# Leaving out the filler matmul ahead of each unit's transposes in a neighbourhood-attention stage

## What is computed

```
qkv = (layernorm(x) @ qkv_w + qkv_b)            # q is scaled by hd ** -0.5
attn = einsum('nhijc,nhiajbc->nhijab', q, kwin) + bias
attn = softmax(attn over the 7 x 7 window)
out = einsum('nhijab,nhiajbc->nhijc', attn, vwin)
x = x + out @ proj_w + proj_b
x = x + gelu(layernorm(x) @ fc1_w + fc1_b) @ fc2_w + fc2_b
```

## Time and profile before

| what | value |
|---|---|
| median of 3 runs | 598.47 us (598.18 to 599.26) |
| the profiled execution | 598.55 us |
| its span, first to last instruction | 596.7 us |
| TensorE busy in the span | 518.5 us (87%) |
| VectorE busy | 407.5 us (68%) |
| ScalarE busy | 312.2 us (52%) |
| mean granted TensorE clock | 0.947 |

### The profile page before, as it was taken

How to read it: one execution, slowest core, us unless ns; L and a number is a source line. 1 busy time by engine, 2 the same in 40 slices (tenths; PEclk the granted TensorE clock), 3 DMA queues, 4 the chain that set the end, 5 groups by cost and what they waited for, 6 DMA issues and landing times.

```text
span 596.7 us, 10777 instructions
## 1 busy us (share of the span) xinstructions
PE 518.5 (87%) x4207; PEld 278.9 (47%) x4208; DVE 407.5 (68%) x740; ACT 312.2 (52%) x456; POOL 57.8 (10%) x108
## 2 busy tenths in 40 slices
PE   6898889875899999999999999999999562799871
PEld 5565666641344454444444444444444220366621
DVE  5785676677766568778966886767662456898662
ACT  2764558550365655565556555565556243565440
POOL 8161244211010000100000010000000100000000
PEclk9999999997799999999999999999999966999975
DMA  5101000000000000000000000000000000000001
GB/s 112 41 2 37 1 2 1 2 2 0 1 1 1 1 1 2 1 2 1 0 1 2 2 0 2 11 0 2 1 1 1 1 3 14 1 1 1 1 0 36
DMA packets 9897, 4.37 MB, mean 7 GB/s; under 512 B 8948, under 2 KB 9207, under 8 KB 9847
## 3 DMA queue, kind: packets, MB, share of 16 engines
q1 hardware_dynamic: 8566, 3.66, 2.7%
q10 hardware_dynamic: 1281, 0.01, 0.1%
HBM read 2.09 MB, written 0.52 MB: 4 GB/s over the span
## 4 chain that ended last, share of the span: by engine, by line
PE 71%; DVE 14%; issue 8%; ACT 3%; POOL 2%; SPq 0%; DMA 0%; POOLq 0%; DVEq 0%; ACTq 0%
PE PS L761 18%; PE PS L784 18%; PE PS L745 10%; PE PS L521 2%; PE PS L800 2%; PE PS L728 2%; PE PS L493 2%; PE PS L988 2%; PE PS L505 2%; DVE most L1554 2%; PE PS L683 2%; DVE sbias L1600 2%; PE PS L696 1%; PE PS L594 1%; PE PS L710 1%
## 5 line engine op out<-in xcount | busy, mean ns | idle before, releaser
L1554 DVE TENSOR_REDUCE most<-PS 128x2 f32<-128x1024 f32 x128 | 156.6, 1223 | 75.5 <-PE PS L745 74.5
L1187 ACT ACTIVATE PT<-PS 128x1024 f32<-128x1024 f32 x128 | 131.0, 1024 | 98.6 <-PE PS L761 98.3
L761 PE MATMUL PS<-qS,aS 128*64 128x512 f16 x1024 | 133.7, 383 | 0.0
L784 PE MATMUL PS<-PT,V 128*64 128x512 f32 x512 | 130.8, 592 | 0.0
L745 PE MATMUL PS<-aS,qS 128*64 128x512 f16 x512 | 80.0, 394 | 10.9 <-DVE most L1554 10.4
L761 PEld LDWEIGHTS PS<-qS,aS 128*64 128x64 f16 x1024 | 56.6, 111 | 63.0 <-issue 28.3
L1143 ACT ACTIVATE prob<-sbias,negm 128x320 f32<-128x320 f32 (+1 forms) x64 | 34.3, 538 | 36.5 <-DVE negm L1600 35.8
L745 PEld LDWEIGHTS PS<-aS,qS 128*64 128x64 f16 x512 | 28.1, 112 | 42.0 <-DVE most L1554 18.4
L1306 POOL TENSOR_TENSOR rstd<-var,minus_half 128x8 f32<-128x8 f32 (+1 forms) x9 | 13.6, 1506 | 351.9 <-DVE var L1418 351.9
L784 PEld LDWEIGHTS PS<-PT,V 128*64 128x64 f32 x512 | 35.9, 137 | 23.6 <-issue 0.9
L1600 DVE CUSTOM_DVE_ANT_0 sbias<-PS,PT 128x320 f32<-128x320 f32 (+1 forms) x64 | 28.5, 458 | 3.1 <-PE PS L683 2.9
(11 more groups left out here) (196 smaller groups left out, 682.2 us busy)
## 6 DMA issues: line engine op xcount, KB each, us to landing
xall<-in_x_dram SPq DMA_DIRECT2D x2, 256.0 KB, 4.4
qS<-kS SPq DMA_DIRECT2D x4, 128.0 KB, 2.9
q0M<-kS SPq DMA_DIRECT2D x4, 128.0 KB, 2.4
out_dram<-x SPq DMA_DIRECT2D x4, 128.0 KB, 2.1
w<-in_L_attn_Wq_dram SPq DMA_DIRECT2D x2, 128.0 KB, 2.6
w<-in_L_attn_Wk_dram SPq DMA_DIRECT2D x2, 128.0 KB, 2.8
w<-in_L_attn_Wv_dram SPq DMA_DIRECT2D x2, 128.0 KB, 2.7
fc<-in_L_conv_fc_w_dram SPq DMA_DIRECT2D x2, 64.0 KB, 2.5
```

The lines of the kernel that those rows point to most:

```text
L761: mm = pe.matmul(PS[h0:h0 + C, score_banks(t) + lane, :], aS[:, k0 + h0:k0 + h0 + C], qS[:, part, lane, toks], start=(part == 0), stop=(pa ...
L784: mm = pe.matmul(PS[cols, 6 + g % 2, :], V[:, img * NT + kt, cols], PT[:, g % 2, lane, kt, :], start=(kt == 0), stop=(kt == NT - 1))
L1187: act.activation(PT[:, g % 2, :, phase, :], PS[:, b0:b0 + 2, :], ACT.Exp).then_inc(c1["exped"], 1)
L1554: dve.tensor_reduce(most[:, g % 2, u // 2, u % 2, :], PS[:, 2:4, :], AX.X, ALU.max, negate=True)\
```

## The change

The filler and its helper are left out; nothing else is altered. 64 matmuls and their 64 weight loads go, and the two waits that stood ahead of the filler now stand ahead of the first transpose.

```diff
-FILL = 256
...
-            def keep_busy(bank):
-
-                filler = ident[:, :].bitcast(F16)
-                pe.matmul(bank[:, 0:FILL], filler[:, 0:P], filler[:, 0:FILL], start=True, stop=True)
-
...
                 if u >= 2:
                     pe.wait_ge(c0[half + "_drained"], u // 2)
-                keep_busy(bank)
                 for n, (_, k, _) in enumerate(key_chunks(u // NH0 % NT)):
                     tr = pe.transpose(bank[:, n * P:(n + 1) * P], prob[:, u % 3, n * P:(n + 1) * P], ident[:, :])
```

## The result

The first four runs of the changed kernel took 594.17 us in the median (593.48 to 594.47), those of the kernel before beside them 598.87 us (598.18 to 599.44): a ratio of 0.992 with an interval of 0.9903 to 0.9938. Much of that surplus did not come back when the same kernel was run again. Over all 25 runs of it made here the mean is 595.45 us (593.33 to 597.36, standard deviation 1.2), over the 74 of the kernel before 598.39 us (596.75 to 600.47, standard deviation 0.9): 2.94 us less, with an interval of 2.4 to 3.5 us.

What follows compares the result with a forecast made beforehand. Neighbourhood stage bound by a loop handed between TensorE and VectorE, neither engine full. 598.55 us - 3.0 (fillers on the chain) + 0.3 (later clock rise) = 595.85 us, 595.8 us for the median; range 594.6 to 598.6 us.

Steps and rivals of the forecast that it cites:

- the fillers on the chain: Neighbourhood stage, 26.2 to 131.8 us: 29 filler pieces on the chain that ended last, 3.56 us, upper bound of the gain.
- two corrections: Neighbourhood stage: 0.6 us taken off the gain for scores waiting for their bias, and 0.3 us for a later clock rise.
- A sixth (0.6 us): Neighbourhood stage: taken off the 3.56 us for runs where a score waits for its bias without the filler, leaving 3.0 us.
- The late rise of the clock: Start of the neighbourhood stage: without fillers the rise to the full level may come later, counted at 0.3 us.
- The third rival: Later stages may lie differently to the clock, as at 157.8 us; no own chance, range widened 0.4 us either side.
- The first rival, a short relapse: Neighbourhood stage: clock rises late at the start or falls once behind 88 us, costing 1.8 us: 597.6 us; chance 0.20.
- the idle place at 88 us: Neighbourhood stage: TensorE idle 1.94 us behind the transposes at 87.15 us, waiting for VectorE's layer norm; clock fall there counted nothing.
- The second, VectorE: Neighbourhood stage: VectorE's queued bias, copies and layer norm take the chain over, gain 1.8 us less 0.3: 597.1 us; chance 0.12.
- The sign that was named for it: Neighbourhood stage: the scores' waits for the bias grow by what the waits of copy L341 lose; no size given.
- The fourth, the loss of the full level: Neighbourhood stage: scores alone don't hold the clock, TensorE mostly at 1.2 GHz, 38 us more: 634 us; chance 0.10.
- The signs that were named: No filler rows, transposes behind second score, VectorE's waits below 15.6 us, shift L814 2.7 us earlier, full clock from before 34 us.

Runs made afterwards that it cites:

- The doubled filler: The kernel before with two fillers a unit instead of one: 602.19 us (6 runs), ratio 1.0065.

## Why the prediction was right, and where it was wrong

**The mechanism was right, and that the sum came so close is luck.** The net gain was put at 2.7 us, nearly all of it from the fillers on the chain. The stage became 2.72 us shorter in the first profile, and the mean of all runs 2.94 us, which puts the changed kernel at 595.45 us against the forecast of 595.8 us. The doubled filler measured the term from the other side: 3.59 us, where the chain had counted 3.28 us in the stage and 3.56 us in all. But the 2.7 us hold two corrections that were both off and cancel, and the mean of the runs holds the falls of the clock, which the sum had put at nothing.

**Its two corrections were off, in opposite directions.** A sixth (0.6 us) was taken off for runs in which a score comes to wait for its bias. Of the chain's 3.56 us, 0.84 us did not come back. The stage of the first profile lost 2.72 of the 3.28 us that it held; for the other 0.56 us the waits of the scores for VectorE, which grew by 2.3 us, are the likely place, as foreseen; that was not traced piece by piece. The piece of 0.28 us behind the last score brought nothing: at 17.07 us of the lower level the stretch from there to the first product with the values is 35.31 us before and 35.31 to 35.48 us after. From the first unit to the middle one (unit 32) the stage lost 47.62 - 45.54 = 2.08 us of the 2.29 us on the chain, from there to the last 51.23 - 50.59 = 0.64 us of 0.99. The late rise of the clock, put at 0.3 us, did not come. The first eight units, most of them before the rise, became 0.38 us shorter (7.76 to 7.38 us; 7.36 to 7.39 us in all five profiles), about the 0.42 us that the two fillers at the lower level held on the chain. The version without fillers in the first half did have a late rise (two transposes at 31.51 us still took 0.63 us, and that is 4.4 us behind its second unit's score at 27.11 us), and took 7.69 us for these units, 0.31 us more; so the term exists, but not in every execution.

**The step that failed is the spread of a measurement, and with it the lower end of the range.** The third rival, a later stage that lies differently to the clock, was priced at "0.4 us on either side, about what the three runs differ". Three runs that lay within 1.08 us of each other were taken for the spread; 74 runs span 3.7 us. The rise between the stages was allowed one us; it moved by 3.4 us. The profiles show the draws: 0.8 to 1.2 us for the start of the stage, which the prediction did not have at all, and one more or one less stretch of 3.4 us at the lower level between the stages, 0.7 to 0.9 us from the last score to the first global product with the values. The first comparison had both on the good side in the profile of the changed kernel and both on the bad side in that of the kernel before, and none of its four runs had a clock of 0.944 or less, which 11 of 25 have. A range with these two draws in it would have gone down by 0.8 + 0.7 us below the chain's 595.0 us, not by 0.4.

**The first rival, a short relapse, came true beside the forecast and not in its place.** The clock fell behind the idle place at 88 us, as it said, in two of five profiles, and at 74 us in two more. Its chance of 0.20 was low for a fall that four of five profiles show; what was held against it, that the fillers are a small part of the stretch, was no safeguard. The price was put at 1.8 us, on the reckoning that the next run of TensorE would take twice as long; it was 0.84 to 1.24 us, and the clock was back after 3.4 us. It ate 31 to 46% of the stage's 2.72 us, not two thirds.

**The second, VectorE, holds in part.** The sign that was named for it appeared: the scores' waits for the bias grew by 2.3 us, and those of L341 lost 2.2 us. Yet VectorE did not take the chain over, since the stage still gave 2.72 of 3.28 us, so the sign tells nothing of the size. The rival shows in the second half of the stage and in the unequal prices of a filler added and a filler removed.

**The fourth, the loss of the full level, is refuted.** Outside the short falls the clock stood at 1.00 through the stage without a single filler. By the rule of the Trainium skill's page "TensorE: Matmul & The Clock Gate" (section on the PE-mode transpose), that transposes don't count as activity for the clock in the way other matmuls do, this rival was taken up; the 38 us that it would have cost did not come. Whether the rule has a part in the short falls is not shown: scores, transposes and products are mixed everywhere in the stage.

**The signs that were named:** no filler rows, transposes right behind the second score, and waits of VectorE for transposes below 15.6 us (13.4) came true. The full level to the end of the stage came true in one profile of five. The global stage's shift began 4.5 us earlier (146.6 instead of 151.1 us) and not 2.7: it lies behind the two draws of the execution and was a poor marker.

**Still open.** From the first global product with the values to the end, all five profiles of the changed kernel are 0.2 to 0.5 us shorter than the three of before. All of it lies in the routed steps: the global stage, from its first product with the values to its last, took 307.7 us in all eight. Behind it the changed kernel took 128.25 to 128.42 us and the kernel before 128.63 to 128.80, but five of the other versions took from 127.29 to 129.05 us there (the trace of the doubled filler lacks rows at that place), so that this difference need not be the change's. How often the clock falls in the stage without fillers, and what makes it fall, stays open too. Nor was it found out why one DMA issue of SyncE sometimes takes more than twice its usual time.

## What to carry to other kernels

A filler matmul that stands between two handovers of a loop costs time wherever the chain passes through it. Its pieces on the chain of the kernel before (3.28 us in the stage) bound the gain of leaving it out from above, and 2.72 us came of it; the falls of the clock that the fillers had held off took a part back. The same kind of matmul placed where its engine waits for another costs next to nothing and, where it keeps the clock up, brought 2.1 to 3.0 us. Where the granted clock changes several times in a run, take the spread from many runs before giving a range, and compare two profiles milestone by milestone, so that what the execution drew is not credited to the change.

## What was unexpected in the hardware

The clock fell behind a stretch that TensorE's rows covered for 2.67 of 3.40 us (71.0 to 74.4 us), and did not fall in other executions of the same program at the same place. One issue of a DMA on SyncE took 0.59 or 0.60 us or, in seven of the fourteen profiles, 1.08 to 1.57 us, and moved the start of a stage with it.
